# Attention's second half on blocks of two tiles, and ring sums in four PSUM banks, in the first gather stage of a graph network

## The reference, cut to what matters

```
xn = _layernorm(x, axis=-1)
x = x + _L0_gnn_ref(xn, edge_index, ...)      # sum of xn[src] into dst, W1, batch norm, W2
      + _L0_mix_ref(xn[None], ...)[0]         # linear attention with RMS norms
# inside _L0_mix_ref (8 heads):
q = elu(q) + 1.0;  k = elu(k) + 1.0
kv = einsum('bnhd,bnhm->bhdm', k, v)
z = 1.0 / (einsum('bnhd,bhd->bnh', q, k.sum(axis=1)) + EPS_ATTN)
out = einsum('bnhd,bhdm,bnh->bnhm', q, kv, z) # then @ w_out + b_out, added to xn, RMS norm
```

## Time and profile before

| | |
|---|---|
| median of 3 runs | 2961.8 us (2961.68 to 2962.96) |
| the profiled execution's own time | 2957.87 us |
| its span, first to last instruction | 2956.3 us |
| mean granted TensorE clock | 0.957 |
| TensorE, busy | 2620.8 us (89%) |
| GpSimd, busy | 1801.7 us (61%) |
| VectorE, busy | 1693.5 us (57%) |
| ScalarE, busy | 1438.3 us (49%) |
| gathers of g1 (L893) | 702, from 57.6 to 953.3 us |

### The profile page before, as it was taken

One profiled execution on the slowest core, in us unless ns is written; L12 is line 12 of the kernel. 1 busy time (PEld: TensorE's weight loads), 2 busy tenths in 40 slices (PEclk: granted clock), 3 DMA queues, 4 the chain that ended last, 5 costly groups with the idle time before them and its releaser, 6 DMA issues. The chain is left out here.

```text
span 2956.3 us, 53086 instructions
## 1 busy us (share of the span) xinstructions
PE 2620.8 (89%) x14911; PEld 2213.7 (75%) x14911; DVE 1693.5 (57%) x5328; ACT 1438.3 (49%) x4034; POOL 1801.7 (61%) x1937
## 2 busy tenths in 40 slices
PE   2999988999898899699995989999888888789998
PEld 1787777888788788588874766666677777678887
DVE  6632233887666666645554656666666767634333
ACT  4122222463222555245657978787667856422222
POOL 5777777777776255446666777777777777500000
PEclk9999999999999999799997999999999989989999
DMA  8464445777666476445555444444456655532222
GB/s 235 128 183 138 139 138 162 242 223 237 212 216 200 146 239 218 131 125 160 163 156 162 132 136 128 137 127 140 121 177 188 184 158 159 152 107 71 78 74 59
DMA packets 292630, 464.33 MB, mean 157 GB/s; under 512 B 89497, under 2 KB 224578, under 8 KB 291260
## 3 DMA queue, kind: packets, MB, share of 16 engines
q1 hardware_dynamic: 210392, 238.09, 26.9%
q0 software_dynamic: 81216, 221.98, 25.5%
q10 hardware_dynamic: 750, 1.08, 0.1%
HBM read 349.16 MB, written 111.83 MB: 156 GB/s over the span
## 5 line engine op out<-in xcount | busy, mean ns | idle before, releaser
L2614 POOL DMA_INDIRECT g_got<-xm_d,idx x782 | 768.2, 982 | 249.1 <-issue 234.8
L893 POOL DMA_INDIRECT g_got<-xn_d,idx x702 | 683.0, 973 | 228.5 <-issue 209.0
L2226 PEld LDWEIGHTS ps<-g_hotw,g_got 128*128 128x128 f32 x3128 | 410.1, 198 | 211.7 <-DMA g_got<-xm_d,idx 138.6
L2226 PE MATMUL ps<-g_hotw,g_got 128*128 128x128 f32 (+11 forms) x3128 | 437.0, 289 | 139.9 <-DMA g_got<-xm_d,idx 134.5
L1292 PE MATMUL ps<-g_hot,g_got 128*128 128x120 f32 (+4 forms) x2808 | 376.6, 281 | 63.0 <-DMA g_got<-xn_d,idx 62.7
L1292 PEld LDWEIGHTS ps<-g_hot,g_got 128*128 128x128 f32 x2808 | 357.9, 196 | 97.8 <-DMA g_got<-xn_d,idx 77.6
L2669 ACT ACTIVATE g_hotw<-g_hot,g_wr 128x16 f32<-128x16 f32 (+8 forms) x1308 | 298.2, 312 | 19.7 <-DVE g_hot L600 19.3
L1479 POOL TENSOR_TENSOR p_ln_rs<-p_ln_pre,neg_half 125x2 f32<-125x2 f32 x50 | 35.1, 701 | 437.8 <-DVE p_ln_pre L1474 437.8
L2759 DVE TENSOR_TENSOR g_ring<-g_ring,ps 128x84 f32 (+10 forms) x391 | 133.0, 340 | 233.1 <-PE ps L2226 170.7
L1105 DVE TENSOR_TENSOR g_ring<-g_ring,ps 128x40 f32 (+9 forms) x351 | 73.2, 209 | 291.2 <-PE ps L1292 274.0
L2110 POOL DMA_INDIRECT z_d<-p_yj,p_to x108 | 126.9, 1175 | 139.2 <-DVE p_to L2146 119.6
(11 more groups left out here) (387 smaller groups left out, 4923.1 us busy)
## 6 DMA issues: line engine op xcount, KB each, us to landing
h_d<-gin_hid SPq DMA_DIRECT2D x23, 1000.0 KB, 5.4
gin_hid<-h_d SPq DMA_DIRECT2D x23, 1000.0 KB, 5.8
job_in<-jobs_d SPq DMA_DIRECT2D x54, 258.0 KB, 3.0
g_got<-xm_d,idx POOLq DMA_INDIRECT x782, 3.3
g_got<-xn_d,idx POOLq DMA_INDIRECT x702
p_z<-z_d SPq DMA_DIRECT2D x49, 224.0 KB
q_d<-g_qo SPq DMA_DIRECT2D x25, 250.0 KB, 2.8
g_xa<-xn_d SPq DMA_DIRECT2D x50, 125.0 KB
```

What stands on the lines that cost most here:

```text
L893: landed.start(e.indirect_dma_start(got[:, k % (2 * GB), :], None, xn_d[0:N, :], bass.IndirectOffsetOnAxis(ap=idx[:, HT + k:HT + k + 1], a ...
L2226: mm = e.matmul(to, rows[j][:, c * P:(c + 1) * P], hotw[:, j, c * w:4 * w].unsqueeze(1).broadcast_to([P, r, n]), start=(j == 0), stop=(j = ...
L2614: landed.start(e.indirect_dma_start(got[:, 2 * (g % GB) + j, :], None, xm_d[0:N, :], bass.IndirectOffsetOnAxis(ap=idx[:, 2 * g + j:2 * g + ...
```

## The change

Attention's second half is done on blocks of two tiles: 25 items with 14 steps between them in place of 50 with 7. Denominators are one matmul of 250 columns for each half of the features, in place of 125. Reciprocal and quotient are done for each half of the features apart (`divide(0)`, `divide(1)`), each 128x250, the same size as before. Four matmuls of 256 columns make the product of both tiles into the whole of bank 3, for all blocks. The additions and the multiplication by the gate work on 125x512 elements in place of 125x256. Square and gate remain one instruction for each tile. `finish` is parted in two stages, `finish` and `residual`. Loads and stores carry two tiles. `qt` and `qz` lie in the memory of the spent weights `wqkv`. The buffers are two deep (three for `hh`) in place of four, of twice the size. Bank 7, which is free now, becomes a fourth bank for the ring sums once the edge network is through.

```diff
-            GB, HR, SR, LEAD, AR = 12, 7, 2, 10, 4
+            GB, HR, SR, LEAD, AR, HH = 12, 7, 2, 10, 2, 3
...
-            ATT = every(MIX[0], 7, NT)
+            ATT = every(MIX[0], 14, NB)
...
-                return q % 3 if q in AFTER else q % 2
...
-            def out_at(i):
-                return (7, 0) if i >= ALONE else (3, 250)
+                return (0, 1, 2, 7)[q % 4] if q in AFTER else q % 2
...
                     def load_qt(i):
-                        if i < 2:
-                            q_out.wait(e, i, (NB - 1 - i) // 2)
-                        zs.wait(e, i - AR, "qz")
...
+                        if i == 0:
+                            for u in range(2):
+                                q_out.wait(e, u, (NB - 1 - u) // 2)
+                            proj.wait(e, NB - 1, "q")
+                        zs.wait(e, i - AR, "qz1")
+                        qt_in.start(e.dma_start(qt[:, i % AR, :, :], q_d[i].rearrange("p (c n) -> p c n", c=DC)), i % AR)
...
-                             (QKV, [(load_xn, 0), (store_q, 25)]), (ATT, [(store_att, 33), (load_x0, 3), (load_xa, -3), (load_qt, -3)]),
+                             (QKV, [(load_xn, 0), (store_q, 25)]), (ATT, [(store_att, 38), (load_x0, 14), (load_xa, 2), (load_qt, -3)]),
...
-                             (NEAR, [(one_plus, 26), (root, 20), (square, 17), (move_den, 9)]),
-                             (FAR, [(far(one_plus), 27), (far(root), 21), (far(square), 18), (far(move_den), 10)]),
+                             (ATT, [(one_plus, 29), (root, 24), (square, 21), (move_den, 10)]),
...
-                    def divide(i):
-                        moved.wait(e, i, "den")
-                        outs.wait(e, i - 1, "out")
-                        zs.done(e.reciprocal(den[:, :, :], den[:, :, :]), "inv")
-                        zs.wait(e, i, "inv")
-                        zs.done(e.tensor_tensor(qz[:, :, :], qt[:, i % AR, :, :], den[:, :, :], ALU.mult), "qz")
+                    def divide(c):
+                        def stage(i):
+                            moved.wait(e, i, "den")
+                            outs.wait(e, i - 1, "out")
+                            zs.done(e.reciprocal(den[:, c, :], den[:, c, :]), f"inv{c}")
+                            zs.wait(e, i, f"inv{c}")
+                            zs.done(e.tensor_tensor(qz[:, c, :], qt[:, i % AR, c, :], den[:, c, :], ALU.mult), f"qz{c}")
+                        return stage
...
-                        hsum.done(e.tensor_tensor(xa[:, i % AR, :], xa[:, i % AR, :], bout[:, :], ALU.add), "xb")
+                        hsum.done(e.tensor_tensor(xa[:, i % AR, :, :], xa[:, i % AR, :, :],
+                                                  bout[:, :].unsqueeze(1).broadcast_to([TN, 2, D]), ALU.add), "xb")
...
-                        fin.done(e.tensor_tensor(hh[:, i % AR, :], hh[:, i % AR, :], gw[:, :], ALU.mult), "gh")
+                        fin.done(e.tensor_tensor(hh[:, i % HH, :, :], hh[:, i % HH, :, :], gw[:, :, :], ALU.mult), "gh")
+
+                    def residual(i):
...
-                        fin.done(e.tensor_tensor(hh[:, i % AR, :], hh[:, i % AR, :], x0[:, i % AR, :], ALU.add), "y")
+                        fin.done(e.tensor_tensor(hh[:, i % HH, :, :], hh[:, i % HH, :, :], x0[:, i % AR, :, :], ALU.add), "y")
...
-                             (NEAR, [(finish, 29), (invert, 23), (add_h, 15), (divide, 10), (add_xb, 8)]),
-                             (FAR, [(far(finish), 30), (far(invert), 24), (far(add_h), 16), (far(divide), 11), (far(add_xb), 9)]),
+                             (ATT, [(residual, 33), (finish, 32), (invert, 27), (add_h, 18), (divide(1), 12), (divide(0), 11), (add_xb, 9)]),
...
                     def denominators(i):
                         qt_in.wait(e, i % AR, i // AR)
                         moved.wait(e, i - 1, "den")
-                        if i <= ALONE:
-                            hsum.wait(e, i - 1, "h")
+                        hsum.wait(e, i - 1, "h")
...
                     def product(i):
-                        zs.wait(e, i, "qz")
...
+                        zs.wait(e, i, "qz1")
+                        for t in range(2):
+                            for c in range(DC):
+                                mm = e.matmul(ps[0:TN, 3, t * D:(t + 1) * D], qz[:, c, t * TN:(t + 1) * TN], mix[:, c, :],
+                                              start=(c == 0), stop=(c == DC - 1))
...
-                             (MIX, [(mix_out, 3), (mix_turn, 1)]), (NEAR, [(product, 13), (denominators, 8)]),
-                             (FAR, [(far(product), 14), (far(denominators), 8)]),
+                             (MIX, [(mix_out, 3), (mix_turn, 1)]), (ATT, [(product, 15), (denominators, 8)]),
```

More of the change, by code:

```diff
@@ L747, in gps_kernel @@
             fin = ph.steps("fin", "gh", "y")
-            xp_out = ph.landing("xp", AR)
+            xp_out = ph.landing("xp", HH)
             rturn = ph.steps("rturn", "T")
@@ L878, in _ @@
                     timeline(LAST_STEP, ([u - 10 for u in UPS], [(load_own, 0)]), ([WTS[-1] + 10], [(load_edges, 0)]),
-                             (QKV, [(load_xn, 0), (store_q, 25)]), (ATT, [(store_att, 33), (load_x0, 3), (load_xa, -3), (load_qt, -3)]),
+                             (QKV, [(load_xn, 0), (store_q, 25)]), (ATT, [(store_att, 38), (load_x0, 14), (load_xa, 2), (load_qt, -3)]),
                              (UPS[:-2], [(store_h, 20)]), ([QKV[0] + 34], [(load_rest, 0)]))
                     e.wait_ge(s_tables, 2 * 16)
-                    for u in range(AR):
-                        xp_out.wait(e, u, (NT - 1 - u) // AR)
+                    for u in range(HH):
+                        xp_out.wait(e, u, (NB - 1 - u) // HH)
                     for u in range(2):
@@ L929, in move_den @@
                         dens.wait(e, i, "den")
[L930 removed]
+                        zs.wait(e, i - 1, "qz1")
                         if i == 0:
                             e.wait_ge(s_eps, 1)
[L933 to L935 removed]
+                        moved.done(e.activation(den[:, :, :], ps[:, 3, 0:DC * BN].rearrange("p (c n) -> p c n", c=DC),
                                                 ACT.Identity, bias=eps[:, 0:1]), "den")
@@ L955, in one_plus @@
                         fin.wait(e, i - 1, "gh")
-                        gate.done(e.activation(gw[:, :], wn2[:, :], ACT.Identity, bias=ones[0:TN, 0:1],
-                                               scale=rr[:, i % AR:i % AR + 1]), "g")
+                        for t in range(2):
+                            ins = e.activation(gw[:, t, :], wn2[:, :], ACT.Identity, bias=ones[0:TN, 0:1],
+                                               scale=rr[:, i % AR, t:t + 1])
+                        gate.done(ins, "g")
                     def zero(b):
@@ L1287, in sums @@
                             scaled.wait(e, 0, "wr")
+                        if g // 2 in AFTER and bank_of(g // 2) == 7:
+                            silu.wait(e, NV - 1, "silu")
                         r = copies(w)
@@ L1365, in product @@
                     def product(i):
-                        zs.wait(e, i, "qz")
-                        if i == ALONE:
-                            silu.wait(e, NV - 1, "silu")
-                        if i > ALONE:
-                            hsum.wait(e, i - 1, "h")
-                        bank, at = out_at(i)
-                        for c in range(DC):
-                            mm = e.matmul(ps[0:TN, bank, at:at + D], qz[:, c, :], mix[:, c, :],
-                                          start=(c == 0), stop=(c == DC - 1))
+                        zs.wait(e, i, "qz1")
+                        for t in range(2):
+                            for c in range(DC):
+                                mm = e.matmul(ps[0:TN, 3, t * D:(t + 1) * D], qz[:, c, t * TN:(t + 1) * TN], mix[:, c, :],
+                                              start=(c == 0), stop=(c == DC - 1))
                         outs.done(mm, "out")
```

62 lines of the change are left out of this document (26 added, 36 removed).

## The result

| | before | changed |
|---|---|---|
| median | 2962.0 us (8 runs) | 2969.0 us (8 runs, 2965.0 to 2972.4) |
| ratio | | 1.0023, 95% interval 1.0012 to 1.0034 |
| profiled execution | 2957.9 us | 2965.0 us |
| gathers, first to last start | 895.7 us | 898.9 us |
| last gather to the next phase's matmuls | 24.4 us | 26.9 us |

One of the eight runs of the kernel before took 3933.8 us; it is left out of the ratio. The changed kernel is slower by 0.23%. The forecast was 2965.7, the range 2958 to 2971. In a later comparison on another device (e5) the same two kernels stood at 2961.6 and 2967.6, ratio 1.0018 (1.0008 to 1.0028). The change costs about 6 us (5.3 and 6.8 by the two ratios). The two profiled executions differ by 7.1 us, but 1.6 of them lie behind the start of the next phase, where the code is the same.

What follows compares the result with a forecast made beforehand. The prediction took GpSimd's back-to-back gathers to bound the stage. Relief elsewhere, the fourth bank and new waits counted zero; stalls added 3.9 us to the profiled 2957.9, giving 2961.8, and a median of 2965.7 us, range 2958 to 2971.

Steps and rivals of the forecast that it cites:

- GpSimd issues without a break, and all else is cover: In g1's stage gathers run back to back, so work saved on TensorE, VectorE, ScalarE and DMA counts nothing.
- TensorE was to wait more than 62.7 us for rows: A sign to look for: with less to do, TensorE waits longer for gathered rows than the 62.7 us before.
- Longer two-operand instructions stall gathers, 3.9 us: In attention, VectorE instructions with both operands in SBUF hold the shared port; the last gather comes 3.9 us later.
- The model gave 5.1 and 9.0: Estimated stalls of gathers by attention's two-operand instructions: 5.1 us before the change, 9.0 after.
- The upper bound, with the whole length counted: Stalls in attention if an instruction's whole length counted: 16.5 us against 5.1, 11.4 more.
- the gather at 599.97: A gather of 1.42 us, read as 0.47 too long and going on 0.12 us behind L1207's end.
- The tail stays 24 us: From the last gather to the next phase some 24 us in either version, since no attention stands there.
- Waits for the second quotient are paid from the slots: TensorE's waits before attention's product, perhaps 1 to 2 us, eat from 14 us in hand; cost zero.
- The fourth bank: nothing: The extra bank for ring sums gains zero, since no wait of TensorE for an addition is seen.
- The Trainium skill's rule: VectorE and GpSimd share ports as an exclusive lock, held by a VectorE instruction with two SBUF inputs for its whole length.

Runs made afterwards that it cites:

- e5: The changed kernel again, unedited, on another device: 2967.6 us against 2961.6 for the kernel before, ratio 1.0018.
- e3: Kernel before plus 50 VectorE additions of 125x512, both operands in SBUF, on the slower device: 3397.8 us against 3400.3, ratio 0.9995.
- e4: Kernel before plus 50 VectorE batch statistics over 125x512, one operand in SBUF, on the slower device: 3400.0 us against 3400.3, ratio 1.0005.
- e7: Kernel before plus 50 VectorE additions of 125x512, both operands in SBUF, where the kernel before takes 2961.6 us: 2972.1 us, ratio 1.0026.
- e9: Kernel before with long two-operand VectorE instructions in pieces and a semaphore wait between pieces: 2955.3 us against 2962.6, ratio 0.9972.
- e11: Changed kernel with five unread matmuls of 512 columns near the end to keep TensorE busy: 2968.4 us, ratio 1.0015 to the kernel before.
- e8: Kernel before with seven kinds of two-operand VectorE instructions cut into pieces, no waits between: 2956.7 us against 2961.6, ratio 0.9987.
- e6: Changed kernel with bias, gate and addition of x as two instructions of 125x256 each: 2969.5 us, ratio 1.0019 to the kernel before.
- e10: Changed kernel with two-operand VectorE instructions in pieces and waits between pieces: 2961.0 us against 2962.6 for the kernel before, ratio 0.9992.
- e2: Changed kernel with ring sums in three banks, bank 7 unused, on the slower device: 3388.9 us against 3400.3 for the kernel before, ratio 0.9970.
- e12: The kernel before again, unedited, for a second trace: one execution, gathers 897.6 us, tail 24.2 us.

## Why the prediction was right, step by step

*GpSimd issues without a break, and all else is cover.* Right, on devices like the first. The longest wait is 0.3 us in both kernels, and the excess plus 881.6 us gives the length of the run of gathers in eight traces. What TensorE and VectorE saved and the fewer DMAs returned nothing. One sign missed: TensorE was to wait more than 62.7 us for rows, and it waited 61.8. On the slower device the premise fails, and two variants of the change were faster there than before.

*Longer two-operand instructions stall gathers, 3.9 us.* The mechanism held, by the twins e3 and e4, by e7 to e9, and by the count of the stalled gathers. Size: over the two traces of before and the three of the changed order (e11 among them), the gathers take 896.7 and 900.8 us, 4.1 more. Counted by instruction, attention's four lines stall 5.1 and 6.2 us before, 7.4, 8.7 and 9.3 after: 2.8 more. The model gave 5.1 and 9.0. The remaining 1.3 lie outside the changed lines: the scatter of the others, and e5's median gather of 957 ns. That 3.9 meets 4.1 so closely is partly luck, since traces of one and the same kernel differ by 1.9 us (before) and 2.9 (changed). Two details of the working were wrong and changed nothing. The upper bound, with the whole length counted, comes to 17.3 us, 12.2 more than before, and not 16.5 and 11.4. And the gather at 599.97 did not go on 0.12 us behind the end of L1207. That end came 0.59 us into the gather and the gather was 0.47 us too long, so it had been held up 0.12 us after its own start, which is also how the formula uses the number.

*The tail stays 24 us.* Wrong, and the one step that failed: the tail is 24.4 and 24.2 us in the two traces of before, 26.9 and 26.6 in the two of the changed kernel. I had only asked whether attention stood in the tail, not whether the last rows would land as early. These 2.4 us and the 4.1 of the gathers make 6.5, about the 6 that were measured, where the forecast had 3.9. That sum is plausible and not shown. e7 and e8 have tails of 26.0 and 25.7 us in the order of before. And from the next phase to the end, where all kernels have the same code, the ten traces of the faster devices take anything from 1976.2 to 1987.9 us, so single traces can't account for medians to 2 us. The half clock is not the cause, by e11, and by e6, whose tail was 25.6 us at a clock of 1.00 throughout.

*Waits for the second quotient are paid from the slots.* Right for the change: 7.9 us of waits, and 14 tiles behind in place of 13. How near the edge was shows in e10.

*The fourth bank: nothing.* Not contradicted, and hardly tested, since e2 ran only on the slower device and without the unedited changed kernel beside it.

*The Trainium skill's rule* of the shared ports ("SBUF — State Buffer", section "SBUF: two separate sides") agreed in what it says of two SBUF inputs. It says so only against a GpSimd operation that reads SBUF, a condition that the prediction left out; the gather has `idx` in SBUF among its operands. Its section "A bandwidth-pool intuition that's wrong (but worth ruling out)" has the blocked side go on about 115 ns behind the end of VectorE's instruction. No run here shows that: the 0.12 us of 740.51 lie at the start of the gather, and a delay behind the end can't be told from them.

## What to carry to other kernels

Find the engine that never waits and ask what lengthens its instructions, not what is saved beside it. Here fewer and larger instructions on a half-idle VectorE made the stage longer. By the prediction's estimate the mean stall grows with the square of an instruction's length less 0.17 us, and the counts bear it out roughly: 9.0 us estimated against 7.4 to 9.3 counted with the change, 5.1 against 5.1 and 6.2 before. Where GpSimd issues the gathers that pace a stage, cut VectorE's long instructions with both operands in SBUF and leave a wait between the pieces, and count what slots are left before making anything else coarser. What bounds a stage can differ from device to device, as it did here: measure where the kernel will run.

## What was not expected of the hardware

- Pieces issued one behind the other can keep a gather out together: one of 1.65 us waited behind four pieces of 0.28 us (e8). Nine gathers of e8 fared so, 24 others got in between two pieces. With a semaphore wait between the pieces the excess of all gathers went from 10.8 to 6.9 us (e9).
- Who came first is decided some 0.04 us before the gather's start. In the traces of before, changed, e5, e7, e11 and e12, with few exceptions, a two-operand instruction that began by more than that before the gather, and ran on past 0.12 us into it, stalled it. One that began from 0.04 us before to 0.03 us after did not, and was itself longer by up to 0.07 us, as at the earlier trace rows.
- Not only instructions with two tensors stall a gather. Of 12 gathers that L1124 (TENSOR_SCALAR, 125x256, one tensor in SBUF) met in the first trace, eight were longer by 0.02 to 0.14 us. None of the 62 that a reciprocal (L1168) met were, nor any of the 12 that L1181, with one operand in PSUM, met.
- The same program took 2962 us on some devices and 3400 us on another, with TensorE standing up to 4.6 us without any wait that the profile shows.
